# Scaling the softmax rows by a broadcast product instead of a per-row scalar, in a fused attention and gate kernel on one core

## What is computed

```python
scores = jnp.einsum('bkgqd,bksd->bkgqs', qg, k) / math.sqrt(HD)
bias = jnp.where(rel > 0, NEG_INF, slopes[:, :, None, None] * rel)
attn = jax.nn.softmax(scores + bias[None], axis=-1)
out = jnp.einsum('bkgqs,bksd->bkgqd', attn, v)
...
x = x + s * g
```

## Time and profile before

| | |
|---|---|
| median of 3 runs | 3105.32 us (3103.99 to 3113.26) |
| the profiled execution, its own time | 3094.95 us |
| its span, first to last instruction | 3092.9 us |
| mean granted TensorE clock, share of full speed | 0.94 |
| PE, PEld, DVE, ACT, POOL busy | 88%, 77%, 70%, 49%, 55% |
| L1080, VectorE: 512 instructions | 412.1 us busy, 865 ns mean |
| PE waiting for L1065 on DVE (matmul records) | 124.6 us in 59 waits |

### The profile page before, as it was taken

The page is one execution under the profiler, slowest core; times in us unless marked ns, Lnnn a source line. Parts: engine busy times, 40 slices in busy tenths (PEclk is TensorE's granted clock), DMA queues, the critical chain, the costliest instruction groups (busy, mean ns, idle before and its releaser), DMA issues.

```text
span 3092.9 us, 40000 instructions
## 1 busy us (share of the span) xinstructions
PE 2709.7 (88%) x13840; PEld 2374.8 (77%) x13840; DVE 2175.9 (70%) x4132; ACT 1528.9 (49%) x4099; POOL 1714.4 (55%) x821
## 2 busy tenths in 40 slices
PE   3568978888899999999989899999989899999986
PEld 2457767777788788888878788888878788888875
DVE  5357777776777777777777777776777777766776
ACT  2244535454455555555555455555545455556542
POOL 3356556575555655555555656555554655555553
PEclk8779989899999999999989999999999999999998
DMA  7765656656334432333424432333323433333323
GB/s 257 237 236 193 223 191 210 225 205 220 101 116 131 149 108 91 111 96 103 134 72 135 145 106 90 112 110 103 123 83 96 155 121 103 108 103 103 108 67 113
DMA packets 184120, 424.49 MB, mean 137 GB/s; under 512 B 34544, under 2 KB 75632, under 8 KB 183024
## 3 DMA queue, kind: packets, MB, share of 16 engines
q1 hardware_dynamic: 183920, 421.93, 41.8%
HBM read 349.51 MB, written 89.13 MB: 142 GB/s over the span
## 4 chain that ended last, share of the span: by engine, by line
PE 67%; DVE 21%; ACT 3%; DMA 3%; SPq 3%; issue 3%; POOL 1%; DVEq 0%; POOLq 0%; ACTq 0%
PE proj L461 16%; PE proj L462 15%; PE proj L463 15%; DVE prob L1080 9%; PE tr L554 4%; PE sc L461 3%; PE sc L463 3%; PE sc L462 3%; PE ot L462 2%; PE ot L463 2%; PE ot L461 2%; PE tr L534 2%; ACT prob L747 2%; DVE prob L1070 2%; DMA wl<-wu 1%
## 5 line engine op out<-in xcount | busy, mean ns | idle before, releaser
L867 POOL TENSOR_TENSOR wl<-wl,wh 128x896 fp32r<-128x896 f32 x448 | 992.0, 2244 | 1029.2 <-ACT wh L680 1029.2
L461 PE MATMUL proj<-wh,xh 128*128 128x448 f32 x1792 | 694.5, 388 | 128.3 <-DVE raw L1065 73.8
L462 PE MATMUL proj<-wl,xh 128*128 128x448 f32 x1792 | 676.2, 377 | 0.0
L463 PE MATMUL proj<-wh,xl 128*128 128x448 f32 x1792 | 674.9, 377 | 0.0
L461 PE MATMUL proj<-o_hi,wb_hi 128*128 128x512 f32 x1024 | 439.6, 429 | 85.4 <-DVE raw L1065 50.7
L461 PEld LDWEIGHTS proj<-wh,xh 128*128 128x128 f32 x1792 | 351.0, 196 | 173.9 <-DVE raw L1065 86.2
L747 ACT ACTIVATE prob<-prob,negmax 128x128 f32<-128x128 f32 (+3 forms) x512 | 286.7, 565 | 354.7 <-DVE negmax L1070 354.7
L726 ACT ACTIVATE pT_hi<-tr 128x512 fp32r<-128x512 f32 (+3 forms) x512 | 197.5, 440 | 511.6 <-PE tr L554 511.4
L1097 DVE TENSOR_TENSOR acc<-acc,proj 128x512 f32<-128x512 f32 x480 | 327.0, 683 | 174.1 <-PE proj L463 173.2
L878 POOL TENSOR_TENSOR wb_lo<-wb_lo,wb_hi 128x1024 fp32r<-128x1024 f32 x128 | 318.3, 2487 | 224.7 <-ACT wb_hi L690 224.5
L680 ACT ACTIVATE wh<-wl 128x896 fp32r<-128x896 f32 x448 | 406.3, 966 | 71.3 <-DMA wl<-wu 70.7
(11 more groups left out here) (117 smaller groups left out, 4529.2 us busy)
## 6 DMA issues: line engine op xcount, KB each, us to landing
wl<-wu SPq DMA_DIRECT2D x448, 448.0 KB, 4.0
wb_lo<-wo_in SPq DMA_DIRECT2D x128, 512.0 KB, 3.3
wu<-xtok SPq DMA_DIRECT2D x98, 448.0 KB, 3.9
wo_in<-wo SPq DMA_DIRECT2D x32, 512.0 KB, 5.5
xtok<-wa SPq DMA_DIRECT2D x56, 256.0 KB, 4.8
gate_dram<-z_buf SPq DMA_DIRECT2D x32, 256.0 KB, 5.1
xtok<-xT SPq DMA_DIRECT2D x32, 256.0 KB, 4.8
xtok<-gate_dram SPq DMA_DIRECT2D x32, 256.0 KB, 5.6
```

The costliest lines, as they stand in the source:

```text
L461: pe.matmul(out, hi_l, hi_r, start=first, stop=False, skip_group_check=onto)
L462: pe.matmul(out, hi_l, lo_r, start=False, stop=False, skip_group_check=onto)
L463: return pe.matmul(out, lo_l, hi_r, start=False, stop=last, skip_group_check=onto)
L867: pool.tensor_tensor(w_slot(wl, w), w_slot(wl, w, True), w_slot(wh, w), ALU.subtract).then_inc(w_ready, 1)
```

## The change

The four scalings of `normalise` are a multiplication of two tensors. The second tensor is the column of row factors, read with a step of zero over the columns of the tile.

```diff
                 for i in range(NT):
                     p = prob[:, P_AT[i]:P_AT[i] + P * (i + 1)]
-                    ins = dve.tensor_scalar(p, p, rs_inv[:, i:i + 1], None, ALU.mult)
+                    ins = dve.tensor_tensor(p, p, rs_inv[:, i:i + 1].to_broadcast([P, P * (i + 1)]), ALU.mult)
                 ins.then_inc(prob_ready, 1)
```

## The result

The changed kernel took 3117.52 us (median of 15 runs, 3111.38 to 3124.31) against 3105.32 (15 runs, 3095.74 to 3119.51): 12.2 us more, a ratio of 1.0038 with a 95% interval of 1.0026 to 1.0050. It is slower, as forecast, by half of what was forecast (24 us). The interval, 8 to 15.5 us, lies in the forecast's wide range and just under its own bounds of 16 to 33.

A forecast was written before the change was run, and what follows sets the result against it. TensorE is busy 88% of the span, with VectorE's scalings on the path in places. Terms 9.0 + 5.3 + 4.0 + 2.0 + 2.6 + 0.9 = 23.8 us on the 3105.3 median gave 3129 us (+0.77%), range 3106 to 3150.

The forecast's parts named there:

- Step 3: Six early j = 3 steps with 7.14 us groups: +0.67 us each, 4.0 us; three of 9.1 us: 2.0 us.
- Step 5: 27 steps without TensorE waiting for a piece, and first groups' j = 1: nothing lost; 5 us if uncovered.
- step 1: 45 steps with j = 1 or 2 where TensorE waits behind the scalings: +0.20 us each, 9.0 us.
- step 2: 19 j = 3 steps with GpSimd idle and a 0.3 us thin cover: TensorE delayed 0.28 us each, 5.3 us.
- step 4: Three j = 3 steps awaiting keys and the last group's four: 2.6 us; steps 6.1, 14.1, 22.1: 0.9 us.
- The bias pushed behind the products: Rival: all four products pass L886 in j = 1, 2 steps, groups near 3.28 us; 3107 us, no change; 12%.
- Another instruction slips in: Rival: GpSimd's L878 goes ahead of the last product, 2.4 us more in 45 steps; 3237 us; 6%.
- The clock: Rival: TensorE idle times tip steady steps between clock kinds; all slow 3150 us, 8%; all fast 3099 us, 7%.
- All hidden: Rival: thicker cover in steps like 12.3 and only 0.1 in place 1; sum 14 us less, 3115 us; 5%.
- place 1: The same 45 steps as step 1, with j = 1 or 2: +0.20 us each, bounds 0.15 to 0.35.

The follow-up runs named there:

- three-tile run: Against the kernel before, tiles 0 to 2 (128, 256, 384 columns) multiplied as products, the fourth kept as a scaling: 3114.97 us against 3102.73, 1.0038.
- the three runs by step: Kernel before with the product only in steps with j = 3, j = 1 and 2, or j = 0: ratios 1.0018, 1.0002 and 1.0000.
- a third form: Kernel before with each scaling also summing its row into a column nobody reads: 2989.26 us against 3102.73, 0.9631.
- run 409: Not a label of a run: "run" is a verb here, for a 384-column scaling that takes 409 ns inside L886 in the kernel before.

## Why the prediction was right in sign and wrong in size

**Right.** The instruction's price: 1.70 us for a group of four unhindered (1.69 said), 684 ns at 512 columns, the spread operand free. Step 3 of the sum, each scaling waiting for one whole sum of GpSimd: +0.64 us measured, +0.67 said, 6 us in nine steps. Step 5: what lies ahead of a wait for TensorE is swallowed, and the run with j = 0 alone shows it, 1.0000. L1027 in step 12.3 took up VectorE's loss.

**The first step that failed is step 1**, "I take +0.20, nearer the first, since it starts just before L886 ends". The sum had an end without a wait for L886 (+0.15) and one with it (+0.35), and the value taken mixed them. The truth was the first end and a little under it: +0.09, because the last product starts at 2.99 us, not 3.04, and needs 677 ns. What the prediction missed is that a product in the middle of L886 doesn't wait for its end at all. The three-tile run, which puts a scaling back there, gives the 3.81 us of the missing wait. In the sum: 45 x 0.09 = 4.1 us in place of 9.0, and the run with j = 1 and 2 alone (-4 to +5 us) agrees with the one and excludes the other. Both ends were in the text, but no row of a product at the end of a GpSimd scaling. The 0.55 us that L1027 needed behind L878 is the end of a sum, not of a scaling of GpSimd's, and these two hold VectorE in different ways.

**The second is step 2**, 0.28 us "plus the weight load that is no longer hidden". The delay at the second matmul was 0.25 us, as said; but TensorE made up about half of it within the next 6 us, so step 12.3 lost 0.13, and the 15 steady ones 0.19 each: 19 x 0.19 = 3.6 us in place of 5.3. The trace shows how, not why: the 23 matmuls from 1392.56 to 1397.22 come 0.203 us apart, where 0.207 was the pace before; no run was made on it.

With these two, the sum is 4.1 + 3.6 + 6.0 for step 3 and up to 3.5 for step 4, some 17 us, a little above the measured 8 to 15.5. So it is probably still too large, and the three runs by step, 6 us in all, lean that way too. Which term is too large stays open. The last group can't be read for it: it grew by more than its share between the two traces, 17.2 to 18.2 us in two of its steps and 14.3 to 17.1 in the third, at a granted clock of 0.80 to 0.91 for 0.90 to 1.00; with the change in j = 0 alone its steps 31.1 and 31.2, not edited there, grew by 2.4 us as well.

**The rivals.** The bias pushed behind the products: partly. Its premise, that products follow each other closer than scalings, is not in the rows: four scalings overlap by 0.08 to 0.09 us at a seam, and so do the products. Yet L886 was passed by one product more than before and grew to 1.86 us, not 3, and took its front's toll on the 384-column product. Another instruction slips in: not here, for the 0.56 us that L886 outlasts the last product's start, but in both kernels with a short L886. The clock: it moved the counts of slow steps by 0 and 1 here, and so the rival did not decide this result. Yet the prediction's account of it was wrong: it priced the clock only as a chance of all or nothing (+21 or -30 us) and did not ask how long TensorE's idle time must be. A path gain of 3 us brought 25.

**All hidden**, which gave 3115 us, is nearest in number. Its two halves were a thicker cover in step 12.3, which is not what happened (the 0.25 us delay is there), and 0.1 in place 1, which is.

What the forecast didn't ask is whether another form would be rid of the waits. It had read from the rows that GpSimd makes the group of 3.58 us so long, and then looked only for what the new form adds. Of these 3.58 us 2.3 are waits for GpSimd (1.27 are left with GpSimd idle), and a third form, at 1.95 wherever it stands, avoids them: 113 us, nine times what the change costs.

## What to carry to other kernels

Where a VectorE instruction takes much longer than the same form elsewhere, read what GpSimd does beside it before counting columns: the choice of form decides whether it waits, and the slower form can be the faster one (742 ns for 479, and 3.7% off the kernel). Price such a choice by each instruction's start against the neighbour's begin and end, and take one end or the other, not the middle. And where equal steps fall now to one and now to another granted clock behind an idle time of TensorE, try shortening that idle time a little: here 0.14 us in 22 steps, 3 us on the path, were worth 25.

## What the runs showed of the hardware

- A GpSimd scaling of 512 columns (L886, 1.56 us alone) holds VectorE's scalings off at its front (0.46 us) and at its end (0.35 us), and lets a 384-column one run 409 ns in between. VectorE's product is held off only at the front (964 ns for 550, 384 columns): 677 ns, unhindered, across its end. The Trainium skill ("SBUF — State Buffer", section "SBUF: two separate sides") calls this an exclusive lock for the whole instruction. For GpSimd's sums (L867, L918, L878) the traces agree; for its scaling they don't.
- VectorE's scaling with an accumulator takes 347, 475, 608 and 742 ns for 128, 256, 384 and 512 columns, and the read of its sum another 83 ns, beside the next; these are means over all 128 of each, most of them beside work of GpSimd.
- Taking work from GpSimd made the kernel 67 us slower (3169.86 for 3102.73, a single run), by letting its next instruction in ahead of one of VectorE: the group of step 12.1 grew from 3.58 to 4.96 us.
- TensorE idle for 1.67 instead of 1.81 us in most of 22 steps: 25 us less, none of the 15 steady steps with j = 1 of the slow kind, and 22.5 us less busy time for the same matmuls. Why 6 of 15 equal steps fall to 0.93 with 1.81 us, and 9 do not, stays open.
- Half of a delay of 0.25 us was made up by TensorE within 6 us in step 12.3: its matmuls came 0.203 us apart instead of 0.207. Over the 15 steady steps like it, a quarter was made up.
